# Three-pass value products in the second attention of a two-layer gated block, with scores three key tiles ahead and the value-output products moved in front of the token transposes

## What is computed

```python
q = rmsnorm((_layernorm(x) @ Wq).reshape(B, Sq, H, D), gq)
k = rmsnorm((ctx @ Wk).reshape(B, Skv, H, D), gk)
v = (ctx @ Wv).reshape(B, Skv, H, D)
attn = softmax(einsum('bqhd,bkhd->bhqk', q, k) / sqrt(D), axis=-1)
x = x + tanh(g_xattn[1]) * (einsum('bhqk,bkhd->bqhd', attn, v).reshape(B, Sq, H * D) @ Wo)
```

## Time and profile before

| | us |
|---|---|
| median of 3 runs (lowest to highest) | 2025.71 (2024.62 to 2027.47) |
| the profiled execution | 2027.91 |
| its span, first to last instruction | 2025.8 |
| PE / DVE / ACT / POOL busy in the span | 1876.0 / 1171.5 / 1042.1 / 322.7 |
| mean granted TensorE clock | 0.966 |

### The profile page before, as it was taken

The page is one execution under the profiler, slowest core; times in us unless marked ns, Lnnn a source line. Parts: engine busy times, 40 slices in busy tenths (PEclk is TensorE's granted clock), DMA queues, the critical chain, the costliest instruction groups (busy, mean ns, idle before and its releaser), DMA issues.

```text
span 2025.8 us, 29157 instructions
## 1 busy us (share of the span) xinstructions
PE 1876.0 (93%) x8765; PEld 1280.9 (63%) x8767; DVE 1171.5 (58%) x1894; ACT 1042.1 (51%) x1705; POOL 322.7 (16%) x294
## 2 busy tenths in 40 slices
PE   5889898959998899999999999999999998999998
PEld 3444444548886666666666666666666666788886
DVE  8565656246666664456644566444574445666665
ACT  2566667713333565556655566555665554333332
POOL 3010101024442200000000000000000002444542
PEclk9899999969999899999999999999999997999999
DMA  3422314064452110000100001000000001354453
GB/s 91 102 52 68 84 35 97 7 200 109 115 118 50 33 33 0 0 0 1 33 0 0 0 1 33 0 0 0 0 1 0 0 0 37 82 113 109 110 116 77
DMA packets 110124, 96.56 MB, mean 48 GB/s; under 512 B 72836, under 2 KB 94472, under 8 KB 109416
## 3 DMA queue, kind: packets, MB, share of 16 engines
q1 hardware_dynamic: 110056, 95.67, 19.2%
HBM read 73.73 MB, written 1.44 MB: 37 GB/s over the span
## 4 chain that ended last, share of the span: by engine, by line
PE 80%; DVE 10%; SPq 2%; ACT 2%; issue 2%; POOL 2%; DMA 1%; ACTq 0%; DVEq 0%; POOLq 0%
PE ps L1146 18%; PE ps L1083 17%; PE ps L390 16%; PE ps L401 8%; PE ps L963 4%; PE ps L950 4%; PE ps L1160 3%; PE ps L1094 3%; SPq L491 2%; DVE s_rk L1657 2%; PE ps L897 2%; POOL s_stage L713 1%; PE ps L1118 1%; PE ps L1155 1%; DVE s_rq L1653 1%
## 5 line engine op out<-in xcount | busy, mean ns | idle before, releaser
L860 ACT ACTIVATE s_p<-ps,s_g,s_rk 128x256 f32<-128x256 f32 (+1 forms) x832 | 417.7, 561 | 299.2 <-PE ps L1083 269.2
L1083 PE MATMUL ps<-s_qq,s_ctxT 128*128 (+2 forms) x1248 | 500.1, 514 | 2.7 <-ACT s_ksq L834 2.7
L1146 PE MATMUL ps<-s_p,s_ctx 128*128 128x512 f32 (+1 forms) x832 | 418.0, 596 | 12.8 <-ACT s_p L860 12.8
L1689 DVE TENSOR_TENSOR s_dsum<-s_dsum,s_p 128x512 f32<-128x512 f32 (+1 forms) x384 | 265.9, 693 | 235.6 <-ACT s_p L860 223.9
L1083 PEld LDWEIGHTS ps<-s_qq,s_ctxT 128*128 128x128 f32 (+1 forms) x1248 | 231.7, 186 | 200.9 <-issue 164.1
L390 PE MATMUL ps<-s_xT,s_wgus 128*128 128x512 f32 x1440 | 350.3, 392 | 3.2 <-DVE s_hw L1585 2.9
L390 PEld LDWEIGHTS ps<-s_xT,s_wgus 128*128 128x128 f32 x1440 | 271.9, 189 | 62.2 <-DVE s_hw L1585 3.7
L778 ACT ACTIVATE s_p<-ps,s_bsm 128x1024 f32<-128x1024 f32 x208 | 219.6, 1111 | 96.9 <-PE ps L963 85.5
L1146 PEld LDWEIGHTS ps<-s_p,s_ctx 128*128 128x128 f32 (+1 forms) x832 | 157.3, 189 | 76.8 <-ACT s_p L860 24.6
L401 PE MATMUL ps<-s_hs,s_wds 128*128 128x512 f32 x720 | 184.6, 392 | 1.8 <-DVE s_hs L1587 1.8
L1587 DVE TENSOR_TENSOR s_hs<-s_hw,s_hs 128x512 fp32r<-128x512 f32 x120 | 137.1, 1143 | 82.6 <-ACT s_hs L333 82.6
(11 more groups left out here) (245 smaller groups left out, 1836.4 us busy)
## 6 DMA issues: line engine op xcount, KB each, us to landing
s_wB<-w1s SPq DMA_DIRECT2D x64, 256.0 KB, 3.9
s_kT<-s_kst SPq DMA_DIRECT2D x96, 128.0 KB, 2.4
s_kT<-s_kst SPq DMA_DIRECT2D x96, 80.0 KB, 2.1
s_wB<-w0s SPq DMA_DIRECT2D x16, 384.0 KB, 3.6
s_wB<-w0s SPq DMA_DIRECT2D x16, 256.0 KB, 4.0
s_wgu<-in_L_ffn_Wg_dram SPq DMA_DIRECT2D x64, 64.0 KB, 2.9
s_wgu<-in_L_ffn_Wu_dram SPq DMA_DIRECT2D x64, 64.0 KB, 2.7
s_wd<-in_L_ffn_Wd_dram SPq DMA_DIRECT2D x64, 64.0 KB, 2.5
```

Source lines behind the costliest of these rows:

```text
L860: ins = nc.scalar.activation(p1[0:r, BANK1[t], j, :], ps[0:r, BANK1[t], j * SQ:(j + 1) * SQ], ACT.Exp, bias=g1[0:r, 3:4], scale=rk_col(t, ...
L1083: ins = nc.tensor.matmul(out, lhs(x_), rhs(y_), start=first and n == 0, stop=last and n == 2)
L1146: nc.tensor.matmul(ps[:, 4, :], ctx1[0:ROWS1[t], t, :], p1[0:ROWS1[t], BANK1[t], :, :].rearrange("p a n -> p (a n)"), start=t == 0, stop=t ...
L1689: v.tensor_tensor(dsum[0:r, :], dsum[0:r, :], pt[0:r, :], ALU.add).then_inc(s.summed, 1)
```

## The change

**Value products.** A new table names ten of the thirteen tiles (`SPLIT1`: 0, 1, 2, 4, 5, 6, 8 to 11). Their weights are split into hi and lo in a ring of five pairs of buffers, `ps1`: ACT rounds seven of the tiles behind their exponentials, DVE rounds three (2, 6, 10), DVE subtracts all ten. `ctx1` gets a low part too, subtracted by POOL once for each batch. V of these tiles is three fp32r passes; V of tiles 3, 7 and 12 stays plain fp32 and reads a copy, `ctxw`. The first copy into `dsum` and the first sum become one addition of tiles 0 and 1.

**Order in the pair loop.** Scores run three tiles ahead, V one tile behind them; the next pair's first three scores stand ahead of this pair's last values. `p1` gets a fourth ring buffer (`SLOT1`). DVE's reciprocal and scaled additions of a pair (`finish`) move into the next round, behind its tile 2.

**Around the loop.** The `m1` products stand ahead of the token transposes, in banks 0 to 3, and ACT, no longer DVE, copies them out, ahead of its square root. ACT copies the second half of `yT` at both mixtures' ends while DVE copies the first. The unscaled queries `q1` lie in `p1` instead of `stage`, so the next batch's context may be loaded earlier. The rounding of Wk moves ahead.

```diff
+SLOT1 = [t % 4 for t in range(KT - 1)] + [4]
+SPLIT1 = (0, 1, 2, 4, 5, 6, 8, 9, 10, 11)
+HI_DVE = (2, 6, 10)
+RING1 = 5
...
             for tt in range(NT):
+                if tt % TB == 0:
+                    pool.wait_ge(s.ctx_kept, 3 * (tt // TB) + 1)
+                    st = stage[:, KV:].rearrange("p (t c) -> p t c", c=C)
+                    g_.tensor_tensor(ctx1[:, 1], st[:, 0:KT - 1, :], ctx1[:, 0].bitcast(F32), ALU.subtract).then_inc(s.ctx_low, 1)
...
-            act_turn(act, 2)
             act.wait_ge(s.w1_loaded, 16 * 7)
             nc.scalar.copy(wk1[:, 0, :], stage[:, 0:H1 * D1]).then_inc(s.wk_hi, 1)
+            act_keep(act, 0)
+            for j in range(8):
+                act.wait_ge(s.m1_made, j + 1)
+                nc.scalar.copy(m1[:, 2 * j:2 * j + 2, :].rearrange("p h n -> p (h n)"), ps[:, j % 4, :]).then_inc(s.m1_read, 1)
+            act_turn(act, 2)
...
-                        act.wait_ge(s.pv1, primed(at(k, hp, KT, t - 2 if t >= 3 else t - 3)))
-                        act.wait_ge(s.summed, primed(at(k, hp, KT, t - 2 if t >= 3 else t - 3)))
+                        slot_free(act, b, hp, t)
...
                         ins.then_inc(s.probs1, 1)
+                        if t in HI_ACT:
+                            pair_free(act, b, hp, t)
+                            act.wait_ge(s.probs1, primed(at(k, hp, KT, t + 1)))
+                            nc.scalar.copy(ps1[:, SPLIT1.index(t) % RING1, 0, :], p1[:, SLOT1[t], :, :].rearrange("p a n -> p (a n)")).then_inc(s.p_hi, 1)
...
+                def values1(hp, t):
+                    if t == 0:
+                        pe.wait_ge(s.o1_read, primed(hp + 8 * b))
+                    first, last = t == 0, t == KT - 1
+                    if t in SPLIT1:
+                        n = SPLIT1.index(t)
+                        pe.wait_ge(s.p_lo, primed(hp * len(SPLIT1) + (len(SPLIT1) * 8 * b + n + 1)))
+                        ins = product(ps[:, 4, :], lambda part: ctx1[:, part, t, :], lambda part: ps1[:, n % RING1, part, :], first, last)
...
                 def pair(hp, following):
                     for t in range(KT):
-                        if t + 2 < KT:
-                            scores1(hp, t + 2)
...
-                    if following:
-                        scores1(hp + 1, 0)
-                        scores1(hp + 1, 1)
-                    pe.wait_ge(s.summed, primed(hp * KT + (k0 + KT)))
+                        if t + 3 < KT:
+                            scores1(hp, t + 3)
+                        elif following:
+                            scores1(hp + 1, t + 3 - KT)
+                        if t:
+                            values1(hp, t - 1)
+                    values1(hp, KT - 1)
+                    pe.wait_ge(s.summed, primed(hp * (KT - 1) + ((KT - 1) * 8 * b + KT - 1)))
...
+                        if t in SPLIT1:
+                            hi, lo = (ps1[:, SPLIT1.index(t) % RING1, part, :] for part in range(2))
+                            if t in HI_DVE:
+                                pair_free(dve, b, hp, t)
+                                v.tensor_copy(hi, pt).then_inc(s.p_hid, 1)
...
+                            v.tensor_tensor(lo, pt, hi.bitcast(F32), ALU.subtract).then_inc(s.p_lo, 1)
+                        if t == 2 and not first:
+                            finish(hp)
```

More of the change, by code:

```diff
@@ L60 @@
 BANK1 = [t % 3 for t in range(KT - 1)] + [3]
+SLOT1 = [t % 4 for t in range(KT - 1)] + [4]
+SPLIT1 = (0, 1, 2, 4, 5, 6, 8, 9, 10, 11)
+HI_DVE = (2, 6, 10)
+HI_ACT = tuple(t for t in SPLIT1 if t not in HI_DVE)
+WHOLE1 = (3, 7, 12)
+RING1 = 5
 KSQ = 7
@@ L72 @@
 PRIMED = ("k_sq_read probs0 pv0 o0_read misc_read h1_made h_made hs_hi hs_lo down_done "
-          "probs1 pv1 summed den_made den_read o1_read y1_added scores0 scores1").split()
-PRIME = 4
+          "probs1 pv1 p_hi p_hid p_lo summed den_made den_read o1_read y1_added scores0 scores1").split()
+PRIME = 8
 def primed(count):
@@ L298, in program @@
             "q1_made q1_read q1_var q1_std q1_normed q1_turned q1T_ready qq_made qq_hi qq_read "
-            "scores1 probs1 pv1 summed o1_read den_made den_read y1_made y1_added").split()}
+            "scores1 probs1 p_hi p_hid p_lo ctx_low pv1 summed o1_read den_made den_read y1_made y1_added").split()}
         s = type("Sems", (), S)
@@ L407, in pe_turn_back @@
             for half in range(2):
-                pe.wait_ge(s.yT_kept, 2 * f + half + 1)
+                pe.wait_ge(s.yT_act if half else s.yT_kept, f + 1)
                 for t in range(4):
@@ L1163, in pair @@
                     ins.then_inc(s.y1_made, 1)
-                scores1(0, 0)
-                scores1(0, 1)
+                for t in range(3):
+                    scores1(0, t)
                 with pe.Fori(0, H1 // 2 - 1) as hp:
@@ L1634, in _ @@
             v.tensor_scalar(g1[:, 3:4], g1[:, 3:4], 0.0, -1.0, ALU.max, ALU.mult).then_inc(s.bound1_ready, 1)
-            for j in range(8):
-                dve.wait_ge(s.m1_made, j + 1)
-                v.tensor_copy(m1[:, 2 * j:2 * j + 2, :].rearrange("p h n -> p (h n)"), ps[:, 4 + j % 4, :]).then_inc(s.m1_read, 1)
             for b in range(B):
```

128 lines of the change are left out of this document (80 added, 48 removed).

## The result

The changed kernel takes 1977.3 us (median of four runs, 1975.6 to 1977.8) where the kernel before took 2025.2 beside it: a ratio of 0.976, 95% interval 0.9745 to 0.9779, or 48 us less. The forecast was 1970, the range 1953 to 1997. The profiled execution took 1977.05 us, its span 1974.9; it is compared with the 2025.8 of before.

What follows compares the result with a forecast made beforehand. PE was taken to bound every pair, before and after the change. Loops 47, ahead of batch 0 7 and end 2.2 us sum to 56, off the profiled 2027.9: 1972, so a median of 1970, range 1953 to 1997.

Steps and rivals of the forecast that it cites:

- What bounds a pair: Pair loop: PE bounds a pair before and after, 22.83 us falling to 21.25; DVE and ACT keep up.
- DVE's round: DVE in a pair: 18.2 us of work, 19.4 with the wait for the last V, against PE's 21.25.
- rival (a): Pair loop: DVE pays 0.78 us for each operation, a pair takes 22.7, total about 2013; chance 0.04.
- The rule of the Trainium skill: DVE: next operation starts only once the pipe is empty, so both distances, 0.61 and 0.78 us, would be the longer.
- A V pass at 0.2267: Split V in a pair: three passes take 0.68 instead of 0.854 us, gaining 0.174 a tile, 1.74 a pair.
- rival (c): Split V: three passes cost as much as two fp32 instructions, 0.285 us each; total about 2023; chance 0.02.
- rival (d): V passes at 0.2133 us, nothing lost at the starts, m1 at its better bound: 1952; chance 0.04 with below.
- The uncovered copy: End of a pair: next scores no longer cover DVE's copy to oT1, losing 0.16 us a pair.
- The edges of a batch: Per batch: 12.6 us from eight pairs, + 0.2 and - 0.4 at the last pair, - 0.7 at the start: 11.7.
- Ahead of batch 0: Front, before batch 0: queries start 7.0 to 8.7 us earlier, perhaps at half clock; bounds 5.3 and 8.7, 7 taken.
- The end: Kernel's end: with ACT's copy beside DVE's, the second update follows after 1.5 instead of 3.7 us, 2.2 less.
- The sum: Whole kernel: 47 from the loops, 7 ahead of batch 0 and 2.2 at the end, 56 us less.

Runs made afterwards that it cites:

- the second probe: Changed kernel followed by S-like and V-like fp32r passes behind its last update, some in a loop with register addresses: 0.2267 us for a pass.
- order alone: Changed kernel with nothing split, all thirteen V plain fp32: 2020.3 us in one execution.
- the cover given back: Changed kernel with the next pair's third scores issued behind the last V: 1967.9 us, ratio 0.9715 to the kernel before.
- the dummy passes: Changed kernel with 18 fp32r passes into an unused bank between a batch's third scores and its first pair: 1967.9 us, ratio 0.9722.

## Why the prediction was right, and where its terms were off

**What bounds a pair**: right. PE was the bound before and is it after, with 21.37 of 21.44 us busy; DVE and ACT keep up. DVE's round was put at 18.2 us of work and came to 18.6 (with 0.79 of idle time in it, 0.51 of it for ACT), and it stands idle for 2.85 ahead of its copy. From the timeline of DVE in the changed kernel, the starts that carry this:

```profile
778.68 0.69 DVE L1776 COPY s_oT<-ps 128x512 f32<-128x512 f32 x1 [2.85 <-PE ps L1197]
779.33 0.69 DVE L1772 TENSOR_TENSOR s_ps<-s_p,s_ps 128x512 fp32r<-128x512 f32 x1
779.94 0.69 DVE L1760 TENSOR_TENSOR s_dsum<-s_p 128x512 f32<-128x512 f32 x1
780.54 0.69 DVE L1772 TENSOR_TENSOR s_ps<-s_p,s_ps 128x512 fp32r<-128x512 f32 x1
...
796.59 0.69 DVE L1763 TENSOR_TENSOR s_dsum<-s_dsum,s_p 65x512 f32<-65x512 f32 x1 [0.20 <-ACT s_p L902]
```

0.60 to 0.61 from start to start, as at the single place from which it was read the earlier trace rows, and not 0.78: rival (a) has no footing. The rule of the Trainium skill that the prediction set against this reading (VectorE: DVE Perf Modes, The DRAIN you can't avoid) has an exception that the prediction left out: "A next op that is not held starts earlier". These starts, 0.60 behind a record of 0.69, agree with the exception. The change sets a subtraction between two sums nearly everywhere, so that few operations wait for the one right ahead of them.

**A V pass at 0.2267**: mis-sized, and this is the largest error. The prediction had two values, 0.233 from S in this very loop and 0.2267 from the second mixture, and took the lower because S has an address from the loop's register and V has none. V and S come at the same price, also in the last pairs, which are written out, and the second probe's register changed nothing. Weight loads of a V and the S behind it in the middle of a pair of the changed kernel, and of its last split V and the plain V behind it:

```profile
766.80 0.65 PEld L1129 LDWEIGHTS ps<-s_ps,s_ctx 128*128 128x128 f32 x3
767.49 0.65 PEld L1129 LDWEIGHTS ps<-s_qq,s_ctxT 128*128 128x128 f32 x3
...
776.69 0.66 PEld L1129 LDWEIGHTS ps<-s_ps,s_ctx 128*128 128x128 f32 x3
777.39 0.42 PEld L1197 LDWEIGHTS ps<-s_p,s_ctxw 65*128 65x128 f32 x2
```

So a product takes 0.69 to 0.70 and a pass 0.230 to 0.234, 0.232 on average over the pair, near the 0.231 of the difference above, and neither rival (c)'s 0.285 nor rival (d)'s 0.2133. Thirty passes by 0.0053 is 0.16 a pair, or 5 us in all. With 0.233 the prediction's own sum was 21.44, what was measured; that it meets it to the hundredth is luck, since 0.233 is a little high and the copy below a little low. The nearest row was that of the same loop, and the reason for leaving it was an idea without a row.

**The uncovered copy**: 0.16 predicted, 0.20 to 0.22 measured (order alone 23.05 against 22.83; the cover given back 21.24 against 21.44). With the passes this makes up the 0.19 by which a pair is longer than forecast.

**The edges of a batch**: predicted at 0.9 us lost for each batch, measured about 1.3 at equal clock. At full clock a batch of before takes 19.49 + 6 x 22.83 + 22.83 = 179.3, and one of after, with the dummy passes, 21.18 + 128.67 + 19.63 = 169.5: 9.8 less where eight pairs give 11.1. Some 1.0 of it is lost in the first pair (0.7 predicted) and 0.3 in the last, where V of tile 11 waits for its subtraction; the prediction had the last pair at 19.4 to 19.6 us for that reason, and it took 19.63. The clock has little part in it: half clock in the first pairs costs 1.64 us in three of the four batches before (21.13 against 19.49) and 0.7 to 2.3 in each of the four after (measured against the run with the dummy passes), 4.9 and 5.3 in all. It is a cost that both kernels have, and one that can be taken away.

**Ahead of batch 0**: the steps were right, the sum too low. The queries start 20.07 us behind ACT's last rounding instead of 29.78, 9.7 earlier; predicted were 7.0 to 8.7. The mis-sized step is ACT's: its copies of m1 were put at an end between 658.5 and 660.4 and ended at 657.56, as m1 ran at full clock from 649.77 and ACT's eight copies followed each 0.86 us with PE, so that the norm started at 659.36, 0.2 earlier than before and not 1.0 to 2.8 later; from there to the queries it was 5.50 us and not 5.95. ACT's timeline:

```profile
647.88 1.01 ACT L355 COPY s_wB<-ps 128x1024 f32<-128x1024 f32 x1 [0.66 <-PE ps L434]
650.94 0.58 ACT L845 COPY s_m<-ps 128x512 f32<-128x512 f32 x1 [2.05 <-PE ps L1118]
...
656.98 0.58 ACT L845 COPY s_m<-ps 128x512 f32<-128x512 f32 x1 [0.28 <-PE ps L1118]
657.59 1.28 ACT L321 ACT_TABLE_LOAD   x1
```

That the queries would start at half clock was right (1.3 us), so 8.5 us are left at the first exponential, beside 7 in the sum.

**The end**: 2.2 predicted, 1.95 measured; the two updates now stand in one row, 1.3 us apart in place of 3.7:

```profile
1968.73 2.60 DVE L1849 SCALAR_TENSOR_TENSOR s_x<-ps,s_tg,s_x 128x1024 f32<-128x1024 f32 x2 [1.48 <-PE ps L444]
```

**The sum**: 47 + 7 + 2.2 against 38.6 + 8.5 + 1.95, with 1.9 that no term holds (0.6 ahead of 645 us, 1.5 where batch 2 has its queries at full clock). Of the 8.4 missing in the loops some 6 are the 0.19 a pair, three quarters of them the pass and the rest the copy, 1 to 2 the edges, and 0.4 the half clock, which costs 5.3 and not 4.9. The median lies 7 us above the forecast, well inside the range.

## To carry to other kernels

Three fp32r passes in place of a plain fp32 product save a fifth of its time (0.69 against 0.85 us for 512 columns), as long as rounding (0.62 on ScalarE, 0.455 on VectorE) and subtraction (0.60) have room beside TensorE; where they do not, as with all ten roundings on VectorE, two thirds of the gain go again. If two rows give different prices for the same instruction, take the one from the same loop, unless a third row shows what makes them differ. When scores are brought forward to feed the other engines, keep one product behind the last one that another engine has to read, and fill a known idle time of a few us ahead of a long run of products: here they gave 6 and 5 us in the loops, and two more split tiles 7, each by itself; all three together gave 13 there and not 18.
